# Router logits made expert by expert and turned back; places and counts from summed picks

## The reference

```python
xf = x.reshape(-1, D)                        # 4096 tokens, D = 256
logits = xf @ gate_w + gate_b                # E = 64 experts
top_l, top_i = jax.lax.top_k(logits, K)      # K = 3 choices of a token
gates = jax.nn.softmax(top_l, axis=-1)
oh = jax.nn.one_hot(top_i.reshape(-1), E, dtype=jnp.int32)
pos = (jnp.cumsum(oh, axis=0) * oh).sum(-1) - 1     # place of a choice within its expert
valid = pos < C                              # C = 128 places
buf = jnp.zeros((E, C, D)).at[fe, pos].set(xf[tok], mode='drop')
h = gelu(einsum('ecd,edh->ech', buf, w1) + b1);  y = einsum('ech,ehd->ecd', h, w2) + b2
out = zeros_like(xf).at[tok].add(y[fe, pos] * gates)
```

## Time and profile before

| | us |
|---|---|
| runs shown | 3054.33, 3052.43, 3039.92 |
| median | 3052.43 |
| profiled execution | 3058.41 |
| its span | 3056.7 |
| first routing phase | 17.3 to 120.8 |
| second routing phase | 1303.8 to 1400.0 |

### The profile page before, as it was taken

One profiled execution on the slowest core, in us unless ns is written; L12 is line 12 of the kernel. 1 busy time (PEld: TensorE's weight loads), 2 busy tenths in 40 slices (PEclk: granted clock), 3 DMA queues, 4 the chain that ended last, 5 costly groups with the idle time before them and its releaser, 6 DMA issues. The chain is left out here.

```text
span 3056.7 us, 53879 instructions
## 1 busy us (share of the span) xinstructions
PE 2799.0 (92%) x19171; PEld 1999.8 (65%) x19171; DVE 1706.7 (56%) x4795; ACT 1555.7 (51%) x2621; POOL 1325.4 (43%) x1340
## 2 busy tenths in 40 slices
PE   6899999878988998788999997999879999998999
PEld 5799999733434443467999996666546666655666
DVE  5521212279898888673112212667566666666766
ACT  1233333359999998522333332333267777783332
POOL 4344444369889888363444442300044444320000
PEclk9799999979999999868999997999999999999999
DMA  9299999712222111374999997000142343301000
GB/s 301 80 327 323 329 324 329 221 41 63 61 61 63 48 50 55 103 219 141 330 321 324 328 323 206 1 1 0 38 123 74 78 107 93 88 2 40 14 14 21
DMA packets 307571, 432.88 MB, mean 142 GB/s; under 512 B 29649, under 2 KB 258166, under 8 KB 304246
## 3 DMA queue, kind: packets, MB, share of 16 engines
q1 hardware_dynamic: 281926, 394.86, 40.9%
q0 software_dynamic: 24576, 33.96, 5.2%
q10 hardware_dynamic: 816, 0.79, 0.1%
HBM read 356.47 MB, written 73.07 MB: 141 GB/s over the span
## 5 line engine op out<-in xcount | busy, mean ns | idle before, releaser
L1858 ACT ACTIVATE f_h_t<-f_h_ps,f_b_t 128x128 f32<-128x128 f32 x1024 | 319.4, 363 | 601.8 <-PE f_h_ps L1816 601.8
L2249 POOL TENSOR_TENSOR a_dmg_buf<-a_c 128x2048 f32<-128x2048 f32 x128 | 519.7, 4087 | 68.8 <-PE a_dmg_ps L2313 44.0
L1816 PEld LDWEIGHTS f_h_ps<-f_rows_t,f_w 128*128 128x128 f32 x4096 | 481.5, 193 | 10.1 <-issue 3.5
L1830 PE MATMUL f_y_ps<-f_w,f_h_t 128*128 128x256 f32 x2048 | 485.1, 380 | 0.0
L1816 PE MATMUL f_h_ps<-f_rows_t,f_w 128*128 128x128 f32 x4096 | 482.5, 276 | 2.3 <-DVE f_rows_t L1872 1.2
L1776 POOL DMA_INDIRECT acc_rows<-f_y,f_give x128 | 205.0, 1602 | 492.3 <-DMA acc_rows<-f_y,f_give 450.3
L1830 PEld LDWEIGHTS f_y_ps<-f_w,f_h_t 128*128 128x128 f32 x2048 | 370.8, 191 | 40.3
L1872 DVE COPY f_rows_t<-f_t_ps 128x256 f32<-128x256 f32 x128 | 54.4, 425 | 598.3 <-PE f_t_ps L1804 598.3
L2625 DVE SCALAR_TENSOR_TENSOR a_bond_buf<-a_a,a_small_rep,a_q_ps 128x512 f32<-128x512 f32 x512 | 347.0, 742 | 7.4 <-PE a_q_ps L2443 3.8
L1047 ACT ACTIVATE a_prob<-a_prob,a_neg_top 128x384 f32<-128x384 f32 (+3 forms) x512 | 276.5, 569 | 43.6 <-POOL a_neg_top L866 43.4
L588 DVE SCALAR_TENSOR_TENSOR x_resid<-f_y_ps,f_gate,x_resid 128x256 f32 (+1 forms) x512 | 217.7, 478 | 130.3 <-PE f_y_ps L424 121.9
(11 more groups left out here) (359 smaller groups left out, 4127.3 us busy)
## 6 DMA issues: line engine op xcount, KB each, us to landing
f_w<-in_L_ffn_w_dram SPq DMA_DIRECT2D x256, 1024.0 KB
a_skewed<-skew SPq DMA_DIRECT2D x32, 512.0 KB, 5.4
a_k_s<-parts SPq DMA_DIRECT2D x16, 768.0 KB, 8.0
acc_rows<-x_resid SPq DMA_DIRECT2D x17, 512.0 KB, 9.1
xn_rows<-f_xn SPq DMA_DIRECT2D x16, 512.0 KB, 5.8
a_vals<-val_rows SPq DMA_DIRECT2D x64, 128.0 KB, 2.8
skew<-a_bond SPq DMA_DIRECT2D x128, 64.0 KB, 1.7
x_resid<-acc_rows SPq DMA_DIRECT2D x30, 256.0 KB, 6.9
```

Source lines behind the costliest of these rows:

```text
L1816: last = nc.tensor.matmul(h_ps[n // HB][:, (n % HB) * P:(n % HB + 1) * P], w1_sb[s][:, c, n * P:(n + 1) * P], rows_t[e % 2][:, c, :], star ...
L1830: last = nc.tensor.matmul(y_ps[k][:, 0:D], h_t[k][:, n, :], w2_sb[e % R][:, n, :], start=n == 0, stop=n == HC - 1)
L1858: nc.scalar.activation(h_t[k][:, n, :], h_ps[n // HB][:, (n % HB) * P:(n % HB + 1) * P], ACT.Gelu, bias=b1_t[:, n, e:e + 1]).then_inc(gelu ...
L2249: nc.gpsimd.tensor_tensor(dmg_buf[n % RING][:, :, :], places(c_sb[h], first_place(dg)), c_sb[h][:, PAD:].unsqueeze(1).broadcast_to([P, DG, ...
```

## The change

1. Logits: make_logits takes gate_w (128x64) as weights and streams the 512 tokens of a batch, in two f32 matmuls, into 64 partitions of the bank tp[0]. Experts now lie on the partitions. ScalarE copies the bank to logits_t and adds the bias there, one value for each partition (copy_logits). TensorE turns it back by four transposes of 64x128 (turn_logits) into the bank that VectorE reads as before. In the loop fill_table(i-1) stands between make_logits(i+2) and turn_logits(i+2).
2. Bias: split_bias and its tiles go; gate_b is loaded as a column.
3. Places and counts: VectorE adds the three one-hot rows of a token into picks (two additions in mark); find_places then has 4 matmuls on picks where it had 12 on pick, and count 4 where it had 12.

```diff
+            def make_logits(i):
+                pe.wait_ge(turn_copied, DC * (i + 1))
+                for c in range(DC):
+                    last = nc.tensor.matmul(tp[0][0:E, :], gate_w_sb[:, c, :], xn_t[i % 2][:, c, :],
+                                            start=c == 0, stop=c == DC - 1)
+                last.then_inc(logits_made, 1)
+            def turn_logits(i):
+                pe.wait_ge(logits_copied, i + 1)
                 if i >= 2:
                     pe.wait_ge(logits_read, i - 1)
                 for j in range(TPB):
-                    for c in range(DC):
-                        nc.tensor.matmul(logit_ps[k][:, j * E:(j + 1) * E], xn_t[k][:, c, j * P:(j + 1) * P],
-                                         gate_w_sb[:, c, :], start=c == 0, stop=False)
-                    last = nc.tensor.matmul(logit_ps[k][:, j * E:(j + 1) * E], ones[0:3, :], gate_b_rows[:, :],
-                                            start=False, stop=True)
+                    last = nc.tensor.transpose(logit_ps[i % 2][:, j * E:(j + 1) * E], logits_t[:, j * P:(j + 1) * P],
+                                               core.ident[0:E, 0:E])
                 last.then_inc(logits_ready, 1)
...
-                for r in range(TOP):
-                    nc.tensor.matmul(bank[:, 0:TPB * E], before[:, :], pick[k][:, r, :, :].rearrange("p j e -> p (j e)"),
-                                     start=r == 0, stop=False)
-                for r in range(TOP):
-                    for j in range(TPB - 1):
-                        nc.tensor.matmul(bank[:, (j + 1) * E:TPB * E], ones[:, :],
-                                         pick[k][:, r, j, :].unsqueeze(1).broadcast_to([P, TPB - 1 - j, E]),
-                                         start=False, stop=False)
+                nc.tensor.matmul(bank[:, 0:TPB * E], before[:, :], picks[k][:, :, :].rearrange("p j e -> p (j e)"),
+                                 start=True, stop=False)
+                for j in range(TPB - 1):
+                    nc.tensor.matmul(bank[:, (j + 1) * E:TPB * E], ones[:, :],
+                                     picks[k][:, j, :].unsqueeze(1).broadcast_to([P, TPB - 1 - j, E]),
+                                     start=False, stop=False)
...
+            def copy_logits(i):
+                act.wait_ge(logits_made, i + 1)
+                if i:
+                    act.wait_ge(logits_ready, i)
+                nc.scalar.activation(logits_t[:, :], tp[0][0:E, :], ACT.Identity,
+                                     bias=gate_b_sb[:, 0:1]).then_inc(logits_copied, 1)
...
             root(0)
             copy_turned(0)
+            act.wait_ge(b_loaded, 16)
+            copy_logits(0)
             root(1)
             copy_turned(1)
+            copy_logits(1)
             root(2)
             for i in range(B):
                 exps(i)
...
                 number_tokens(i)
+                if i + 2 < B:
+                    copy_logits(i + 2)
...
+                nc.vector.drain()
+                nc.vector.tensor_tensor(picks[k][:, :, :], pick[k][:, 0, :, :], pick[k][:, 1, :, :], ALU.add)
+                nc.vector.drain()
+                nc.vector.tensor_tensor(picks[k][:, :, :], picks[k][:, :, :], pick[k][:, 2, :, :], ALU.add).then_inc(picks_ready, 1)
```

More of the change, by code:

```diff
@@ L1290, in route @@
         gate_w_sb = sb("gate_w", [P, DC, E])
[L1292 to L1296, removed]
+        gate_b_sb = sb("gate_b", [E, 1])
+        logits_t = sb("logits_t", [E, S])
         iota_e = sb("iota_e", [P, E])
@@ L1315, in route @@
         pick = [sb(f"pick{k}", [P, TOP, TPB, E], BF16) for k in range(2)]
+        picks = [sb(f"picks{k}", [P, TPB, E], BF16) for k in range(2)]
         product = sb("product", [P, TOP, TPB, E])
@@ L1335, in route @@
         before_ready = sem("r_before")
-        bias_split = sem("r_bias_split")
         var_ready = sem("r_var")
@@ L1343, in route @@
         turn_copied = sem("r_turn_copied")
+        logits_made = sem("r_logits_made")
+        logits_copied = sem("r_logits_copied")
         logits_ready = sem("r_logits")
@@ L1349, in route @@
         pick_ready = sem("r_pick")
+        picks_ready = sem("r_picks")
         pos_ready = sem("r_pos")
@@ L1377, in _ @@
             sp.dma_start(gate_w_sb[:, :, :], gate_w.rearrange("(c p) e -> p c e", p=P)).then_inc(w_loaded, 16)
-            sp.dma_start(gate_b_sb[:, :], gate_b.partition_broadcast(3)).then_inc(b_loaded, 16)
+            sp.dma_start(gate_b_sb[:, :], gate_b.rearrange("(e o) -> e o", o=1)).then_inc(b_loaded, 16)
             for i in range(B):
@@ L1453, in turn @@
                         pe.wait_ge(turn_copied, DC * (i - 1) + c + 1)
+                        if c == 0:
+                            pe.wait_ge(logits_copied, i)
                     for j in range(TPB):
@@ L1475, in find_places @@
                 bank = pos_ps[k]
-                pe.wait_ge(pick_ready, i + 1)
+                pe.wait_ge(picks_ready, i + 1)
                 if i >= 2:
                     pe.wait_ge(pos_read, i - 1)
-                for r in range(TOP):
-                    nc.tensor.matmul(bank[:, 0:TPB * E], before[:, :], pick[k][:, r, :, :].rearrange("p j e -> p (j e)"),
-                                     start=r == 0, stop=False)
-                for r in range(TOP):
-                    for j in range(TPB - 1):
-                        nc.tensor.matmul(bank[:, (j + 1) * E:TPB * E], ones[:, :],
-                                         pick[k][:, r, j, :].unsqueeze(1).broadcast_to([P, TPB - 1 - j, E]),
-                                         start=False, stop=False)
+                nc.tensor.matmul(bank[:, 0:TPB * E], before[:, :], picks[k][:, :, :].rearrange("p j e -> p (j e)"),
[4 more added lines that the diff above has]
+                                     start=False, stop=False)
                 if i:
@@ L1495, in count @@
                 nc.tensor.matmul(count_ps[0:1, 0:E], ones_row[:, 0:1], base_row[:, :], start=True, stop=False)
[L1496 to L1499, removed]
+                for j in range(TPB):
+                    last = nc.tensor.matmul(count_ps[0:1, 0:E], ones[:, 0:1], picks[k][:, j, :],
+                                            start=False, stop=j == TPB - 1)
                 last.then_inc(counted, 1)
@@ L1515, in _ @@
             pe.wait_ge(consts, 1)
-            pe.wait_ge(bias_split, 1)
-            find_logits(0)
+            make_logits(0)
+            turn_logits(0)
             turn(1)
-            find_logits(1)
+            make_logits(1)
+            turn_logits(1)
             pe.wait_ge(before_ready, 1)
@@ L1526, in _ @@
                     turn(i + 2)
-                    find_logits(i + 2)
+                    make_logits(i + 2)
                 if i:
                     fill_table(i - 1)
+                if i + 2 < B:
+                    turn_logits(i + 2)
             fill_table(B - 1)
@@ L1594, in inverse_std @@
                 nc.vector.reciprocal(rstd[:, a * TPB:b * TPB], std[:, a * TPB:b * TPB]).then_inc(rstd_ready, 1)
[L1596 to L1611, removed]
             def choose(i):
@@ L1691, in _ @@
             statistics(1, 2)
-            split_bias()
             inverse_std(1)
```

2 lines of the change are left out of this document (removed).

## The result

| us | before | after |
|---|---|---|
| median | 3051.59 | 3060.85 |
| lowest to highest | 3038.79 to 3060.98 | 3056.43 to 3064.94 |
| runs | 20 | 20 |
| span of the profiled execution | 3056.7 | 3063.1 |

The ratio is 1.0035, with a 95% interval of 1.0022 to 1.0047: 9.3 us slower, where +9 was forecast. That the two figures are alike proves little, since the forecast was a sum of terms of both signs. So the routes come first, cut at the same events of the trace: the first BATCH_NORM_STATS of a route, MAX8 of choose(1), MAX8 of choose(7), and the end of the last instruction on give.

A forecast was written before the change was run, and what follows sets the result against it. One chain: a route's end moves the program's end; TensorE bounds the route at the low clock, VectorE at the high. Starts cost 17.4 us, intervals gain; between +14.5 and +3.5, +9 was taken: 3061.5 us, range 3044 to 3077.

The forecast's parts named there:

- The start: First two batches of each route: ScalarE's roots wait behind the logits copies; choose(1) 8.7 us late, 17.4 in all.
- TensorE's interval at the low clock: Places to places in a route's middle: falls from 12.6 to 10.3 us by cheaper logits, places and counts.
- some 6.6: TensorE's interval per batch at the high clock: falls from 8.05 us to some 6.6, so VectorE sets the pace.
- The additions: VectorE's mark gets two additions and drains: 0.7 us a batch, between 0.5 and 1.0, interval 7.93 to 8.6.
- Rival 2: VectorE's mark: POOL holds each addition 0.9 us, interval 10.4 at either clock; +25 us, 3077; chance 0.12.
- What the additions bring back: TensorE's places and counts, 4 matmuls left of 12 each: gains of 1.2 and 0.5 us a batch at the low clock.
- The clock: TensorE's level in both routes: +14.5 us if all low, +3.5 if high after the start; middle taken, +9.
- The middle of the routes: The six intervals from choose(1) to choose(7), both routes together: forecast at -8.4 us.
- The end: Behind choose(7): +0.7 us for additions, about as much less for the CAST; nothing, plus or minus 1 per route.
- Rival 3: Route starts: high clock, and one of two waits on ScalarE costs nothing; -5 us, 3048; chance 0.09.

The follow-up runs named there:

- e10: The kernel after with ScalarE's roots ahead of the logits copies and POOL's entries waiting for the summed picks; 3033.68 us.
- e11: The kernel after with ScalarE's roots ahead of the logits copies, the old places and counts and no additions, rerun in one series with e9 and e10; 3024.76 us.
- e9: The kernel after with only ScalarE's roots moved ahead of the logits copies, rerun in one series with e10 and e11; 3042.10 us.
- e3: The kernel before with the additions, places and counts on picks, and the old logits and bias; 3053.50 us, ratio to before 0.9997.
- e2: The kernel after with the old places and counts on pick and without the additions; 3044.39 us, ratio to before 0.9964.
- e4: The kernel after with ScalarE's roots ahead of the logits copies, the old places and counts and no additions; 3023.90 us, ratio to before 0.9904.
- e6: The kernel before with an unused pair of 512-column matmuls added ahead of each batch's logits on TensorE; 3055.93 us, ratio to before 1.0034.
- e1: The kernel after with root(1) and root(2) moved ahead of copy_logits(0) and copy_logits(1) on ScalarE; 3041.76 us, ratio to before 0.9958.

## Why the prediction came out near, step by step

- **The start: right, a little small.** Forecast 8.7 late in each route and 17.4 in all, with choose(0) near 41 and choose(1) near 52; found 9.4 and 18.8, with 40.98 and 52.80. Removing it gave 19 to 20.5 us. The biased copy took 0.68, not 0.58, each time.
- **TensorE's interval at the low clock: right.** Forecast 10.3, found 10.29. In the second route it is 10.57, at a clock of 0.51. Its parts: matmuls of logits 3.67 (3.54 forecast), transposes 0.69 (0.54; 0.46 at the high level), and the copy hidden by the table. At the high level it is 6.38, for "some 6.6".
- **The additions: the term "I take 0.7" left out the hold.** Freed from POOL, they cost 0.56 us a batch net of what they save on TensorE (e10 to e11), which is near 0.7. Held, the first took 0.90 in the mean of 16 and the second 0.32, 1.2 us in all with drains not counted. Rival 2 came true in part: the hold came in 7 of 16 batches and for the first addition alone, not 0.9 for each, and cost 8.4 us (e9 to e10). Its cause was named, but as a case of all or nothing with a chance of 0.12, where the code shows that POOL's entries wait for the very pick on which the additions start. In all the additions cost 17.3 us net (e9 to e11), 1.1 a batch.
- **What the additions bring back: about nothing here.** Of their gain of 1.7 us on TensorE 1.5 is seen at the low clock (e3: 11.15), but with the new logits TensorE waits for VectorE. The prediction saw VectorE as the bound only at the high clock and kept the gain in its low-clock half.
- **The clock: the middle between the levels was taken, and the gain of the logits was too small.** The middle of the routes was forecast at -8.4 for both routes and came at -9.7. That is luck, near only because the new logits gained more, and the additions cost more, than reckoned: without additions (e2) the middle is 11.7 and 8.3 us shorter than before, 20 in all. With the hold removed (e10) the six intervals take 50.1 and 51.0 us, no more than the 51.6 that the prediction had for the high level alone, though the clock is 0.81 and 0.73: VectorE sets them. So the forecast was 5.5 us too slow by the clock (+9 for +3.5) and 8.4 too fast by the hold. The term's fault is to treat the clock as given, between two bounds, while it moved with what was in the loop: in the second middle 0.67 before, 0.50 in e3, 0.89 in e4, 0.95 in e6.
- **The end: forecast at nothing, plus or minus 1; found +0.1 and +1.6.** In e4 it is 14.4 and 14.0, in e10, without the hold, 14.8 and 15.1. So the hold is part of it.
- **Rival 3** (one wait at the start costs nothing, since the pairs come at the high clock) is out: both pairs ran at 3.33 and 3.67.

In medians of one series: new logits with the roots first -31.9 (before to e4), the queue's order +20.5 (e4 to e2), the additions +17.9 (e4 to e1), together +6.5 if they add; measured +9.3. The remaining 2.8 us is less than before itself moved between series, 3049.1 to 3055.8.

## What to carry to other kernels

An instruction that waits, put into an in-order queue ahead of one that feeds three other engines, costs its whole wait: look first at what stands behind it, since two lines in another order were worth 19 us here, and the matmuls that the summed picks save gave no gain by themselves (e3). Before work is moved to an engine, read who else wakes on the same event; an addition that starts with the neighbour's instruction took 1.60 us for 0.29, and a later wait for the neighbour removed it. And measure a change's parts alone: here one part was worth -32, and two others took back more than all of it.

## What was not expected of the hardware

- TensorE at 93% busy with small matmuls and weight loads stayed at the low clock, 0.50, for a stretch of 60 us (e3), while before's loop with a 512-column pair added to each batch, at 92% busy, had 0.95 (e6). A high busy share did not go with the high clock here. The kernels with a 512-column pair in each batch had it, with fewer matmuls in the loop too (e4: 324 for 351, 0.89 for 0.67).
- Less work on TensorE did not make it faster: with a third of places' and counts' matmuls left, the second route's middle went from 55.6 to 60.1 us at the old logits and the clock from 0.67 to 0.50. The additions came in with it, so the removal alone is not shown to be the cause.
- VectorE and POOL hold each other up to the end of a TENSOR_TENSOR that started first: 1.60 for 0.29 on VectorE, 2.00 for 0.67 and 2.55 for 1.22 on POOL. Behind POOL's f32 TENSOR_SCALAR the additions took at most 0.49.
